# Tail of a mixture of experts: the order of the last sums, and which chunk of tokens is normed first

## The chip, the cores and the metric

The kernel runs on one core of a Trainium2 chip, in one launch. Its time is device microseconds of that core, from the runs shown: the median of three was 709.67 us (709.59 to 709.87). Engines are named as the profile names them: PE is TensorE (PEld its weight loads), DVE is VectorE, ACT is ScalarE, POOL is GpSimd, SP is SyncE, which here only issues DMAs.

## What is computed

Two layers of a perceiver-like model over 512 tokens (8 x 64) of width 256. Each of the six steps adds to the residual `x`. The change lies where the third step ends and the fourth begins:

```python
x = x + _L0_ffn_ref(_layernorm(x), keys, w1, b1, w2, b2, rw, rb)
x = x + _L1_xattn_ref(_layernorm(x), ctx_1024, ctx_1024, mask, gamma, beta)

def _L0_ffn_ref(...):                # mixture: 16 experts, 4 of them for each token
    topv, topi = jax.lax.top_k(logits, TOP_K)
    w = jax.nn.softmax(topv, axis=-1)
    hidden = gelu(jnp.einsum('bld,efd->blef', x, w1) + b1)
    exp_out = jnp.einsum('blef,edf->bled', hidden, w2) + b2
    return jnp.sum(w[..., None] * jnp.take_along_axis(exp_out, topi[..., None], axis=2), axis=2)

def _L1_xattn_ref(q, k, v, mask, gamma, beta):
    logits = jnp.where(mask == 0, NEG, jnp.einsum('bsd,btd->bst', q, k) / 16)
    x = jnp.einsum('bst,btd->bsd', softmax(logits), v)
    return layernorm(x) * gamma + beta
```

## The kernel before, in words

The 512 tokens are four chunks of 128 rows (`TC` = 4), numbered 0 to 3; `X[:, t, :]` is the residual of chunk t. Each engine has its own program, and semaphores alone tie them. Each engine runs its instructions in the order written, so an instruction that waits holds up all behind it on that engine.

**The mixture.** Tokens are sorted by expert into 31 tiles of 128 rows (`TILES`), 8 slices of hidden width each (`UNITS`). PE does the up product of a slice, ACT the gelu, PE the down product, which adds into a bank of `DOWN_BANKS`. The output of tiles 0 to 28 goes to DRAM (`store_tile`, L994) and comes back row by row: `gather_rows(t)` (L999), four indirect DMAs on POOL's queue for each chunk, one for each of a token's four experts. The last two tiles (`LAST` = 2, from `COLD` = 29 on) don't take that way: ACT copies them out (`take_last`, L1292, semaphore `last_taken`), and PE multiplies them with matrices of the tokens' shares (`spreadT`).

**The sums.** Four accumulators, `sums_of(t)`, of 256 columns, two to a bank, take for each chunk the bias (`begin_sums`: gates by `b2`) and the shares of the last two tiles (`add_last(0)` and `add_last(1)`). Before, each of the three does all four chunks at once. `bias_done` counts the banks that are finished: the first holds chunks 0 and 1, the second 2 and 3.

**Chunks become ready on DVE.** `combine(t)` (L1992) is four multiply-adds of gathered rows, `add_sums` (L2020) adds the accumulators, `norm_begin` is the statistics of the layer norm, of which POOL takes the power minus one half (`rstd_of(4, t)`, L702), and `arrive(t)` norms the chunk (L1570) and adds `beta` to the residual (L2027).

**The attention that follows** works chunk by chunk, p = 0 to 3. PE: `turn_tokens` (transposes, L2563), `open_scores` (the mask), `score2` (scores with the context `ctxT2`), `turn2` (transposes of the weights, L2754), `mix2` (product with the context `ctxN2`). ACT: `take_tokens` (copies the transposes, L1256), `weights2` (the exponential, L1329), `take_weights` (L1336). DVE: `greatest` (row maximum, L1998), `normalise` and `leave` (the norm after it and the next layer's). The orders that matter, each of them fixed: DVE has greatest(0), combine(2), greatest(1), arrive(2), combine(3), arrive(3), normalise(0), leave(0), greatest(2). ACT has weights2(2) ahead of take_tokens(3). PE has score2(2), mix2(1), then chunk 3's transposes and score2(3).

**DMAs.** SP issues `ctxT2[2]` (L601) and `ctxN2[1]` (L605), 2 MB each, when all four gathers of chunk 2 have landed, and the last three contexts when `combine(3)` is through and both banks of sums are.

**Filling products.** `keep_running(bank, times)` multiplies constants of 512 columns into a bank that nobody reads. Before, two of them stand behind `add_last(1)`, and one behind `open_scores(0)`.

Of the kernel before, what the change touches and what calls it, by code (L numbers as in the profile page):

```python
# [24 lines left out]
TC = TOK // P  # L25
# [131 lines left out]
def build(nc, d, out):  # L157
    ctx = ExitStack()
    with ctx:
# [536 lines left out]
        def _(pool):  # L696
# [299 lines left out]
            def gather_rows(t, places=range(TOP0)):  # L996
                for j in places:
                    k = TOP0 * t + j
                    nc.gpsimd.indirect_dma_start(y_rows[:, k, :], None, y_slots, bass.IndirectOffsetOnAxis(slots[:, k:k + 1], 0))\  # L999
                        .then_inc(gathered[t], 16)  # L1000
# [16 lines left out]
                pool.wait_ge(y_stored[k], y_stores(k))  # L1017
            gather_rows(0)
            gather_rows(1)
            pool.wait_ge(last_taken, last_before + LAST)  # L1020
            gather_rows(2, range(2))
            rstd_of(4, 0)
            gather_rows(2, range(2, 3))
            rstd_of(4, 1)
            gather_rows(2, range(3, TOP0))
            gather_rows(3)
# [527 lines left out]
        def _(dve):  # L1554
# [431 lines left out]
            for i in range(COLD + 2, TILES):  # L1986
                take_rows(i)

            def combine(t):
                dve.wait_ge(gathered[t], 16 * TOP0)  # L1990
                for j in range(TOP0):
                    order.step(nc.vector.scalar_tensor_tensor(X[:, t, :], y_rows[:, TOP0 * t + j, :], gate_top[:, t, j:j + 1],  # L1992
                                                              X[:, t, :], ALU.mult, ALU.add))

# [28 lines left out]
            def arrive(t):  # L2023

                norm_tile(4, t)
                dve.wait_ge(xn_ready, norm_of(4, t))
                order.mark(nc.vector.tensor_tensor(X[:, t, :], X[:, t, :], part(rows, ROWS, "beta"), ALU.add))  # L2027
# [4 lines left out]
                norm_tile(5, p)  # L2032

            combine(0)
            combine(1)
            add_sums(0, 1)
            norm_begin(4, 0)
            add_sums(1, TC)
            norm_begin(4, 1)
            arrive(0)  # L2040
            arrive(1)
            greatest(0)
            combine(2)
# [236 lines left out]
        def _(pe):  # L2280
# [405 lines left out]
            def sums_of(t):  # L2686
                return pb(SUM_BANKS[t // 2])[:, (t % 2) * D:(t % 2 + 1) * D]

            def begin_sums():
                pe.wait_ge(gateT_ready, 1)  # L2690
                pe.wait_ge(loaded["b2"], 16)
                for t in range(TC):
                    mm(sums_of(t), gateT[:, t, :], b2[:], t % 2 == 0, False)

            def add_last(k):
                pe.wait_ge(last_taken, last_before + k + 1)
                for t in range(TC):
                    done = mm(sums_of(t), spreadT[k][:, t, :], y_tile[(COLD + k) % YB][:], False, k == LAST - 1 and t % 2 == 1)
                    if k == LAST - 1 and t % 2:
                        done.then_inc(bias_done, 1)  # L2700
# [6 lines left out]
            for n in range(TILES * UNITS):  # L2707
                i, u = divmod(n, UNITS)
                if n == REST_AT:
                    dispatch_rest()  # L2710
                if u == (ROW_TURN_AT if i + 1 == HOT else 2) and HOT <= i + 1 < TILES:
                    turn_rows(i + 1)
                if n in SPREAD_AT:
                    turn_spread(SPREAD_AT.index(n))
                if i == COLD and u == 0:
                    turn_gates()
                if i == COLD and u == UNITS - 1:
                    begin_sums()
                if i > COLD and u == UNITS - 2:
                    add_last(i - 1 - COLD)  # L2720
                if n + AHEAD < TILES * UNITS:
                    up(n + AHEAD)
                down(n)

            add_last(LAST - 1)
            keep_running(4, 2)

            def open_scores(p):
                k = p % 2
# [42 lines left out]
                score2(p)  # L2772

            open_scores(0)
            keep_running(4, 1)
            turn_tokens(4, 0, EARLY_BANKS)
            score2(0)
            next_scores(1)
# [372 lines left out]
```

## Time and profile before

| | |
|---|---|
| median of three runs | 709.67 us |
| the profiled execution's own time | 709.58 us |
| its span, first to last instruction | 707.8 us |
| around the span | 1.8 us |
| PE busy | 677.5 us (96%) |
| DVE, POOL, ACT busy | 542.9, 451.5, 413.9 us |
| mean granted clock of PE | 0.998 |

A busy share is an average over stages with different limits. The stage of the change runs from about 478 to 540 us into the span; it is read with the chain of waits, the timelines of the engines, the DMA landings, and the stretches with their granted clock.

### The profile page before, as it was taken

The page shows a single profiled execution, that of the slowest core. Times are in us where ns is not written, and L with a number is a line of the kernel's source. Part 1 is how long each engine was busy: PE and PEld are TensorE (multiplying, and loading weights), DVE is VectorE, ACT ScalarE, POOL GpSimd, SP SyncE. Part 2 cuts the span into 40 slices and gives each one's busy share as a digit, 9 for nine tenths or more (in the row PEclk, how much of TensorE's full clock was granted, in tenths as well). Part 3 has the DMA queues.
Part 4 walks back from the last instruction along what each step waited for, and adds up shares of the span by engine and source line. Part 5 has one row for each costly group of instructions (what it writes and reads, how often), then busy time and mean ns, then how long its engine had stood idle before and what let it go on. Part 6 is the DMA issues. An engine that isn't in the chain of part 4 may idle for free.

```text
span 707.8 us, 15581 instructions
## 1 busy us (share of the span) xinstructions
PE 677.5 (96%) x5734; PEld 556.2 (79%) x5734; DVE 542.9 (77%) x1211; ACT 413.9 (58%) x791; POOL 451.5 (64%) x487
## 2 busy tenths in 40 slices
PE   6899999999999989999999999999999899999998
PEld 3677778777777778999999999997457456666787
DVE  5877878787889766677777777754657999998676
ACT  3665656656665553566666666652346886665441
POOL 4748635556487643798998787736315699898130
PEclk9999999999999999999999999999999999999999
DMA  8301101011006566899998999985874710001000
GB/s 350 124 2 61 61 1 59 2 57 60 0 0 239 210 241 257 295 352 408 421 379 335 352 336 332 351 317 201 332 299 157 258 44 1 1 0 46 1 0 31
DMA packets 20365, 123.38 MB, mean 174 GB/s; under 512 B 2304, under 2 KB 6672, under 8 KB 13008
## 3 DMA queue, kind: packets, MB, share of 16 engines
q1 hardware_dynamic: 17376, 114.59, 42.2%
q0 software_dynamic: 2928, 8.00, 3.1%
q8 instruction: 35, 0.57, 0.3%
q14 instruction: 26, 0.21, 0.1%
HBM read 111.77 MB, written 10.81 MB: 173 GB/s over the span
## 4 chain that ended last, share of the span: by engine, by line
PE 82%; DVE 8%; ACT 5%; issue 2%; POOL 1%; DMA 1%; DVEq 0%; SPq 0%; ACTq 0%; PEldq 0%; POOLq 0%
PE banks L2282 70%; PE banks L2350 8%; DVE shown L2148 2%; PE banks L2918 2%; ACT probs L1156 1%; DVE negmax_raw L1678 1%; PE banks L2591 1%; ACT banks L1449 1%; DVE banks L2155 1%; DVE xn L1570 1%; DMA table<-in_table 1%; PE banks L2754 0%; ACT turned_back L1460 0%; POOL q_heads_hi L714 0%; DVE V L1638 0%
## 5 line engine op out<-in xcount | busy, mean ns | idle before, releaser
L2282 PE MATMUL banks<-xT,raw 128*128 128x128 f32 x992 | 150.5, 275 | 0.6 <-ACT xT L1268 0.6
L2282 PEld LDWEIGHTS banks<-xT,raw 128*128 128x128 f32 x992 | 133.7, 191 | 3.0 <-issue 1.2
L972 POOL TENSOR_TENSOR w_lo<-raw,w_hi 128x1024 fp32r<-128x1024 f32 x52 | 122.8, 2385 | 0.5
L1310 ACT ACTIVATE banks<-banks,later 128x128 f32<-128x128 f32 x208 | 70.5, 339 | 58.3 <-PE banks L2282 57.0
L1942 DVE CAST mid_hi<-banks 128x128 fp32r<-128x128 f32 x208 | 60.0, 289 | 36.5 <-ACT banks L1310 34.4
L1186 ACT ACTIVATE probsT<-banks 128x512 f32<-128x512 f32 x68 | 40.1, 597 | 75.0 <-PE banks L2350 74.7
L1056 POOL TENSOR_TENSOR inject<-BCbc,drive 128x1024 f32<-128x1024 f32 x31 | 72.8, 2362 | 11.3 <-DVE shown L2148 6.5
L1156 ACT ACTIVATE probs<-banks,negmax 128x1024 f32<-128x1024 f32 x64 | 71.2, 1112 | 11.6 <-DVE negmax L1680 9.8
L1678 DVE TENSOR_REDUCE negmax_raw<-banks 128x1 f32<-128x1024 f32 x64 | 77.5, 1211 | 0.5 <-PE banks L2282 0.5
L2282 PE MATMUL banks<-w_hi,mid_hi 128*128 128x256 f32 x208 | 75.5, 363 | 0.0
L2350 PE MATMUL banks<-table,probs 128*128 128x128 f32 x512 | 69.6, 279 | 0.4 <-DVE probsT L1651 0.4
L2350 PEld LDWEIGHTS banks<-table,probs 128*128 128x128 f32 x512 | 55.1, 141 | 16.8 <-issue 14.0
L1944 DVE TENSOR_TENSOR mid_lo<-banks,mid_hi 128x128 fp32r<-128x128 f32 x208 | 60.6, 291 | 7.1
L2282 PE MATMUL banks<-w_hi,mid_lo 128*128 128x256 f32 x208 | 58.6, 282 | 0.0
L2282 PE MATMUL banks<-w_lo,mid_hi 128*128 128x256 f32 x208 | 58.5, 281 | 0.0
L1279 ACT ACTIVATE w_hi<-raw 128x1024 fp32r<-128x1024 f32 x52 | 54.6, 1050 | 0.0
L735 POOL TENSOR_TENSOR ctx_lo<-ctx_raw,ctx_hi 128x1024 fp32r<-128x1024 f32 x14 | 34.3, 2450 | 22.9 <-ACT ctx_hi L1142 22.8
L1449 ACT ACTIVATE banks<-delta,exp_a 128x512 f32<-128x512 f32 x64 | 41.6, 683 | 8.0 <-DVE shown L2165 6.0
L1651 DVE COPY probsT<-banks 128x512 f32<-128x512 f32 x60 | 41.2, 687 | 1.5 <-PE banks L2350 1.5
L1632 DVE SCALAR_TENSOR_TENSOR k_lo<-banks,bk,k_hi 128x512 fp32r<-128x512 f32 x32 | 23.8, 746 | 21.5 <-ACT k_hi L1148 21.5
L2282 PE MATMUL banks<-probsT,V 128*32 128x128 f32 x1024 | 40.0, 277 | 0.0
L2282 PEld LDWEIGHTS banks<-w_hi,mid_hi 128*128 128x128 f32 x208 | 40.0, 192 | 0.0
(363 smaller groups left out, 1710.9 us busy)
## 6 DMA issues: line engine op xcount, KB each, us to landing
raw<-in_w SPq DMA_DIRECT2D x31, 2048.0 KB, 10.6
ctx_raw<-in_ctxT SPq DMA_DIRECT2D x8, 1024.0 KB, 4.8
ctxT<-in_ctxT SPq DMA_DIRECT2D x4, 2048.0 KB, 8.7
ctxN<-in_ctxN SPq DMA_DIRECT2D x4, 2048.0 KB, 13.8
x_slots<-zero SPq DMA_DIRECT2D x1, 3968.0 KB, 12.5
y_slots<-y_tile POOLq DMA_DIRECT2D x29, 128.0 KB, 7.0
wf<-in_w SPq DMA_DIRECT2D x9, 384.0 KB, 6.2
BCbc<-bc_rows SPq DMA_DIRECT2D x6, 512.0 KB, 7.3
```

Source lines behind the costliest of these rows:

```text
L972: nc.gpsimd.tensor_tensor(w2_lo[i % WB][:, cols], raw[i % WB][:, EW // 2:][:, cols], w2_hi[i % 2][:, cols].bitcast(F32), ALU.subtract).the ...
L1056: nc.gpsimd.tensor_tensor(inject[g % 2][:], Bbc[:, GS * g:GS * (g + 1), :], over(drive[:, m, :], GS, 1), ALU.mult).then_inc(inject_ready, 1)
L1156: nc.scalar.activation(probs[i % 2][:], two(i % 2), ACT.Exp, bias=negmax[i % 2][:], scale=0.25, accum_out=sums[i // PAIRS][:, i % PAIRS:i ...
L1279: nc.scalar.activation(w2_hi[i % 2][:, cols], raw[i % WB][:, EW // 2:][:, cols], ACT.Copy).then_inc(w2_hi_ready, 1)
L1310: nc.scalar.activation(to, held, ACT.Gelu, bias=b1[:, bass.ds(at + u, 1)]).then_inc(gelu_done, 1)
L1449: last = nc.scalar.activation(two(HELD_BANKS[g % 2])[:, s * TOK:(s + 1) * TOK], delta[:, m, :], ACT.Copy, scale=exp_a[:, at:at + 1])
L1651: nc.vector.tensor_copy(probsT[c][:, 0:KC // 2, j, :], pb(5).rearrange("p (k n) -> p k n", n=P))\
L1678: nc.vector.tensor_reduce(negmax_raw[i % 2][:], two(i % 2), AX.X, ALU.max, negate=True).then_inc(raw_max, 1)
L1942: nc.vector.tensor_copy(mid_hi[n % HB][:], held).then_inc(mid_hi_ready, 1)
L1944: nc.vector.tensor_tensor(mid_lo[n % HB][:], held, mid_hi[n % HB][:].bitcast(F32), ALU.subtract).then_inc(mid_lo_ready, 1)
L2282: return nc.tensor.matmul(o, lhsT, rhs, start=start, stop=stop)
L2350: last = nc.tensor.transpose(pb(banks[half])[:, k * P:(k + 1) * P], probs[i % 2][:, kc * P:(kc + 1) * P], ident)
```

## The change

It does four things.

1. PE: bias and share sums are made for chunks 0 and 1 first. Those of chunks 2 and 3 come behind, in place of the three filling products; the bias product of chunk 2 stands ahead of the wait for ACT's copy of the last tile.
2. DVE: chunk 0's sums are added as soon as its rows are combined, and it is normed after one of chunk 1's four multiply-adds. The other three follow.
3. DVE: the sums of chunk 1 are added apart (256 columns), those of 2 and 3 together (512) after the statistics of chunk 1.
4. POOL: `rstd_of(4, 0)` stands ahead of the wait for the last tile and of all gathers of chunk 2; before, it stood behind two of them.

```diff
@@ POOL
             gather_rows(1)
+            rstd_of(4, 0)
             pool.wait_ge(last_taken, last_before + LAST)
-            gather_rows(2, range(2))
-            rstd_of(4, 0)
-            gather_rows(2, range(2, 3))
+            gather_rows(2, range(3))
             rstd_of(4, 1)
             gather_rows(2, range(3, TOP0))
@@ DVE
-            def combine(t):
+            def combine(t, places=range(TOP0)):
...
             combine(0)
-            combine(1)
             add_sums(0, 1)
             norm_begin(4, 0)
-            add_sums(1, TC)
+            combine(1, range(1))
+            arrive(0)
+            combine(1, range(1, TOP0))
+            add_sums(1, 2)
             norm_begin(4, 1)
-            arrive(0)
+            add_sums(2, TC)
             arrive(1)
             greatest(0)
@@ PE
                 if i == COLD and u == UNITS - 1:
-                    begin_sums()
+                    begin_sums(range(TC // 2))
                 if i > COLD and u == UNITS - 2:
-                    add_last(i - 1 - COLD)
+                    add_last(i - 1 - COLD, range(TC // 2))
...
-            add_last(LAST - 1)
-            keep_running(4, 2)
+            begin_sums([TC // 2])
+            add_last(LAST - 1, range(TC // 2))
+            begin_sums([TC - 1])
+            for k in range(LAST):
+                add_last(k, range(TC // 2, TC))
...
             open_scores(0)
-            keep_running(4, 1)
             turn_tokens(4, 0, EARLY_BANKS)
```

On PE, around the end of the mixture, before (`b,gateT` is a bias product, `y_tile,spreadT` a share product, `raw,mid` a down product, `later,table` a filling product, `mask_add` opens the scores, `table,xn` are transposes, `ctxT,xnT` the scores):

```order
L2282 MATMUL banks<-raw_123,mid_133 128x256
L2282 MATMUL banks<-y_tile_139,spreadT_178 128x256 x4
L2282 MATMUL banks<-raw_123,mid_134 128x256
L2282 MATMUL banks<-raw_123,mid_135 128x256
L2282 MATMUL banks<-y_tile_140,spreadT_179 128x256 x4
L2282 MATMUL banks<-later,table 128x512 x2
L2282 MATMUL banks<-mask_add_216,ident_r 128x512 x2
L2282 MATMUL banks<-later,table 128x512
L2563 MATMUL banks<-table,xn 128x128 x2
L2282 MATMUL banks<-ctxT_203,xnT 64x512 x8
```

And the same place in the change (lines are one or more further down there):

```order
L2283 MATMUL banks<-raw_123,mid_133 128x256
L2283 MATMUL banks<-y_tile_139,spreadT_178 128x256 x2
L2283 MATMUL banks<-raw_123,mid_134 128x256
L2283 MATMUL banks<-raw_123,mid_135 128x256
L2283 MATMUL banks<-b_53,gateT 128x256
L2283 MATMUL banks<-y_tile_140,spreadT_179 128x256 x2
L2283 MATMUL banks<-b_53,gateT 128x256
L2283 MATMUL banks<-y_tile_139,spreadT_178 128x256 x2
L2283 MATMUL banks<-y_tile_140,spreadT_179 128x256 x2
L2283 MATMUL banks<-mask_add_216,ident_r 128x512 x2
L2564 MATMUL banks<-table,xn 128x128 x2
L2283 MATMUL banks<-ctxT_203,xnT 64x512 x8
```

Two share products ahead of the last down products, and two bias products some way above, moved behind them; the three filling products are gone.

On DVE, from the first combine on, before:

```order
L1992 SCALAR_TENSOR_TENSOR X<-y_rows,gate_top,X 128x256 x8
L2020 TENSOR_TENSOR X<-X,banks 128x256
L1558 BN_STATS stats<-X 128x6
L1562 BN_AGGR moments<-stats 128x2
L1566 TENSOR_SCALAR vareps<-moments 128x1
L2020 TENSOR_TENSOR X<-X,banks 128x768
L1558 BN_STATS stats<-X 128x6
L1562 BN_AGGR moments<-stats 128x2
L1566 TENSOR_SCALAR vareps<-moments 128x1
L1570 TENSOR_SCALAR xn<-X,moments,rstd 128x256
```

In the change:

```order
L1991 SCALAR_TENSOR_TENSOR X<-y_rows,gate_top,X 128x256 x4
L2019 TENSOR_TENSOR X<-X,banks 128x256
L1557 BN_STATS stats<-X 128x6
L1561 BN_AGGR moments<-stats 128x2
L1565 TENSOR_SCALAR vareps<-moments 128x1
L1991 SCALAR_TENSOR_TENSOR X<-y_rows,gate_top,X 128x256
L1569 TENSOR_SCALAR xn<-X,moments,rstd 128x256
L2026 TENSOR_TENSOR X<-X,rows 128x256
L1991 SCALAR_TENSOR_TENSOR X<-y_rows,gate_top,X 128x256 x3
L2019 TENSOR_TENSOR X<-X,banks 128x256
L1557 BN_STATS stats<-X 128x6
```

The norm of chunk 0 (`xn`) moved ahead of three of chunk 1's multiply-adds and of all of chunk 1's statistics.

On POOL, from the last store of a tile on, before (the tenth `y_rows` DMA is the second of chunk 2):

```order
L994 DMA y_slots<-y_tile_138 128x256
L999 DMA y_rows<-y_slots,slots 128x256 x10
L702 TENSOR_TENSOR rstd<-vareps,table 128x1
L999 DMA y_rows<-y_slots,slots 128x256
L702 TENSOR_TENSOR rstd<-vareps,table 128x1
L999 DMA y_rows<-y_slots,slots 128x256 x5
```

In the change:

```order
L994 DMA y_slots<-y_tile_138 128x256
L999 DMA y_rows<-y_slots,slots 128x256 x8
L702 TENSOR_TENSOR rstd<-vareps,table 128x1
L999 DMA y_rows<-y_slots,slots 128x256 x3
L702 TENSOR_TENSOR rstd<-vareps,table 128x1
L999 DMA y_rows<-y_slots,slots 128x256 x5
```

Two gathers moved behind the power for chunk 0; the power for chunk 1 stays between the third and the fourth gather of chunk 2.

## Rows read from the trace of the kernel before

**Rows 1.** The page's chain that ended last: shares of the span by engine

```profile
PE 82%; DVE 8%; ACT 5%; issue 2%; POOL 1%; DMA 1%; DVEq 0%; SPq 0%; ACTq 0%; PEldq 0%; POOLq 0%
```

**Rows 2.** Timeline, PE: start, length, instructions, [idle before, what ended it]

```profile
478.54 1.99 PE L2282 MATMUL banks<-b,gateT 16*128 16x256 f32 x8
...
486.27 1.89 PE L2282 MATMUL banks<-y_tile,spreadT 128*128 128x256 f32 x8
...
489.50 1.99 PE L2282 MATMUL banks<-y_tile,spreadT 128*128 128x256 f32 x8 [0.47 <-ACT y_tile L1292]
491.33 1.88 PE L2282 MATMUL banks<-later,table 128*128 128x512 f32 x4
...
494.37 0.39 PE L2563 MATMUL banks<-table,xn 128*128 128x128 f32 x2
495.32 3.65 PE L2282 MATMUL banks<-ctxT,xnT 128*64 128x512 f32 x16 [0.56 <-ACT xnT L1256]
...
514.67 3.65 PE L2282 MATMUL banks<-ctxN,probsT 128*64 128x256 f32 x32
```

**Rows 3.** Timeline, DVE, the same stretch

```profile
486.66 4.23 DVE L1992 SCALAR_TENSOR_TENSOR X<-y_rows,gate_top,X 128x256 f32<-128x256 f32 x8 [10.78 <-DMA y_rows<-y_slots,slots]
490.92 0.42 DVE L2020 TENSOR_TENSOR X<-X,banks 128x256 f32<-128x256 f32 x1
...
493.86 0.41 DVE L1570 TENSOR_SCALAR xn<-X,moments,rstd 128x256 f32<-128x256 f32 x1
...
506.55 2.05 DVE L1992 SCALAR_TENSOR_TENSOR X<-y_rows,gate_top,X 128x256 f32<-128x256 f32 x4 [0.76 <-DMA y_rows<-y_slots,slots]
...
515.20 1.22 DVE L1998 TENSOR_REDUCE stat<-banks 128x1 f32<-128x1024 f32 x1
```

**Rows 4.** Timeline, POOL: chunk 2's first gather, chunk 0's power, two last gathers

```profile
489.71 0.96 POOL L999 DMA_INDIRECT y_rows<-y_slots,slots  x1 [2.72 <-ACT y_tile L1292]
...
492.29 0.57 POOL L702 TENSOR_TENSOR rstd<-vareps,table 128x1 f32<-128x1 f32 x1 [0.37 <-DVE vareps L1566]
...
494.88 0.99 POOL L999 DMA_INDIRECT y_rows<-y_slots,slots  x1 [0.18 <-issue]
...
499.95 0.95 POOL L999 DMA_INDIRECT y_rows<-y_slots,slots  x1 [0.30 <-issue]
```

**Rows 5.** Timeline, ACT, the same stretch

```profile
489.06 0.38 ACT L1292 ACTIVATE y_tile<-banks 128x256 f32<-128x256 f32 x1 [2.99 <-PE banks L2282]
...
516.64 1.11 ACT L1329 ACTIVATE probs<-banks,stat 128x1024 f32<-128x1024 f32 x1 [5.56 <-DVE stat L1999]
517.65 0.19 ACT L1329 ACTIVATION_READ_ACCUMULATOR probs<-banks,stat 128x1 f32 x1
518.74 0.38 ACT L1256 ACTIVATE xnT<-banks 128x256 f32<-128x256 f32 x1 [0.89 <-PE banks L2563]
```

**Rows 6.** Timeline, SP's queue: the context issued when chunk 2's rows have landed

```profile
498.13 0.46 SPq L605 DMA_DIRECT2D ctxN<-in_ctxN  x1
```

**Rows 7.** Line L605 at 498.0 to 498.3, issue to landing

```profile
DMA to landing us min/median/max: 14.3/14.3/14.3
```

**Rows 8.** Line L999 at 499 to 500 (chunk 3's last gathers), issue to landing

```profile
DMA to landing us min/median/max: 6.6/6.6/6.6
```

**Rows 9.** Timeline, PE, the scores of chunk 3

```profile
519.26 3.65 PE L2282 MATMUL banks<-ctxT,xnT 128*64 128x512 f32 x16
```

**Rows 10.** Stretches: busy PE, PEld, DVE, ACT, POOL; granted clock, DMA share, GB/s

```profile
264.00:266.00 2.00, 1.88 (x12) 1.78 (x12) 1.76 (x14) 1.98 (x4) 0.00 (x0) 0.73 1.05 451
266.00:268.00 2.00, 2.00 (x11) 2.00 (x11) 1.46 (x8) 0.88 (x2) 0.00 (x0) 0.50 0.98 418
268.00:270.00 2.00, 1.81 (x15) 1.62 (x14) 1.11 (x3) 0.00 (x0) 0.00 (x0) 0.92 0.96 401
558.00:560.00 2.00, 0.66 (x3) 0.09 (x1) 2.00 (x3) 2.00 (x5) 2.00 (x2) 1.00 0.98 324
```

**Rows 11.** The page's DMA issues: all 16 gathers, median issue to landing

```profile
y_rows<-y_slots,slots POOLq DMA_INDIRECT x16, 2.8
```

More of the change, by code:

```diff
@@ L1987, in _ @@
                 take_rows(i)
-            def combine(t):
+            def combine(t, places=range(TOP0)):
                 dve.wait_ge(gathered[t], 16 * TOP0)
-                for j in range(TOP0):
+                for j in places:
                     order.step(nc.vector.scalar_tensor_tensor(X[:, t, :], y_rows[:, TOP0 * t + j, :], gate_top[:, t, j:j + 1],
@@ L2687, in sums_of, with begin_sums, add_last @@
                 return pb(SUM_BANKS[t // 2])[:, (t % 2) * D:(t % 2 + 1) * D]
-            def begin_sums():
+            def begin_sums(tiles):
                 pe.wait_ge(gateT_ready, 1)
                 pe.wait_ge(loaded["b2"], 16)
-                for t in range(TC):
+                for t in tiles:
                     mm(sums_of(t), gateT[:, t, :], b2[:], t % 2 == 0, False)
-            def add_last(k):
+            def add_last(k, tiles):
                 pe.wait_ge(last_taken, last_before + k + 1)
-                for t in range(TC):
+                for t in tiles:
                     done = mm(sums_of(t), spreadT[k][:, t, :], y_tile[(COLD + k) % YB][:], False, k == LAST - 1 and t % 2 == 1)
```

## The prediction

> **What bounds the kernel now.** I read the chain that ended last first: 82% of the span lies on PE [rows 1], so a gain must let PE go on sooner. Then PE's own timeline where the change lies [rows 2], then DVE's, POOL's and ACT's for who releases PE [rows 3 to 5], then SP's issues and the landings [rows 6 to 8], because contexts and gathered rows share the DMA engines.
>
> At the end of the mixture PE is dense, then waits 0.47 us at 489.50 for ACT's copy of the last tile, does the share sums, and runs filling products from 491.33 until the transposes of chunk 0 at 494.37 [rows 2]. It fills because DVE delivers chunk 0's norm only at 493.86 to 494.27 [rows 3]: DVE combines chunks 0 and 1 together (eight passes from 486.66, 4.23 us), adds sums, and does chunk 1's statistics before it norms chunk 0. POOL's power for chunk 0 was done at 492.29 + 0.57 = 492.86 [rows 4], one us before DVE used it. So at this point DVE's order bounds PE, by some 3 us.
>
> Further on something else bounds. Chunk 3's multiply-adds start at 506.55, when DVE had stood for its gathered rows [rows 3]. From there DVE's fixed order leads to the row maximum of chunk 2 at 515.20; ACT had stood 5.56 us for it when its exponential starts at 516.64 [rows 5]; and ACT's copy of chunk 3's tokens is queued behind that exponential. Before, that queue is harmless: the copy at 518.74 waits for PE's transposes [rows 5], as PE gets there late.
>
> **The change, part by part.**
>
> *PE, sums split.* Half of the bias products (1.99 us for all) and half of the first share products (1.89) leave the path ahead of the last down product [rows 2]: 1.00 + 0.95 = 1.95 us. The last copy on ACT moves from 489.06 [rows 5] to 487.1. The wait of 0.47 is now covered by one bias product (a quarter of 1.99, 0.50). Share products of chunks 0 and 1 start 0.44 behind the copy's start, as 489.50 did behind 489.06: at 487.55, and need half of 1.99. Their bank is finished at 488.55.
>
> *DVE, chunk 0 first.* The gathers of chunk 0 land before anything that changes, so DVE still starts at 486.66. Four passes, half of 4.23, end at 488.77, 0.2 us after the bank is finished: no new wait. Before, POOL's power started 1.37 us after the sums' add (490.92 to 492.29) [rows 3, 4]; so now at 488.80 + 1.37 = 490.17, done at 490.74. One of chunk 1's passes (4.23/8 = 0.53) fits under that latency. Chunk 0 is normed from 490.78 to 491.19 instead of 494.27: 3.1 us sooner.
>
> *PE, the fillers go.* Behind 488.55 PE still has one bias product and four share products, 0.50 + 0.95 + 1.00, until 491.0, and the mask's products. These have no row here; 491.33 to 494.37 held them and three fillers of up to 1.88/2 each [rows 2], which leaves 0.2 to 0.5. So PE is free at 491.2 to 491.5, just when chunk 0 is there. I take 491.3 for the transposes, 3.1 us sooner, and 492.2 for the first scores (495.32 before). What the fillers kept off, an idle PE, does not arise here, since sums stand in their place.
>
> *POOL, the power ahead of the gathers.* Here the change costs. Gathers of chunk 2 could start at 487.5 now, but POOL stands in line for chunk 0's power until 490.74. The first gather issues at 490.92 (0.18 behind the power, as in the row at 494.88), against 489.71 before [rows 4]. With 0.95 + 0.30 for each, three end at 494.39. Then POOL waits for chunk 1's statistics. DVE: chunk 0's norm ends 491.19, `beta` takes about what an add of 256 columns does, 0.42, so 491.65 with gaps; three passes of 0.53 to 493.24; the sum's add and statistics, again 1.37 until the power starts: 494.61, done 495.18. The fourth gather of chunk 2 issues at 495.36 instead of 494.88: **0.48 us later**. All behind it on POOL's queue is as much later: the last gather of chunk 3 at 500.43 instead of 499.95. On SP's queue the two contexts that wait for chunk 2's rows go out 0.48 later too, and the last three, which wait for chunk 3's combine, as well.
>
> Were chunk 1's statistics in time, the delay would be 0.26 (the three gathers' end at 494.39 alone); were the bank of sums half a us late, it would be 1.0. I take 0.48, since each of its terms has its row.
>
> *What then binds.* Chunk 3's last gather took 6.6 us to land [rows 8], just the 499.95 to 506.55 after which DVE starts [rows 3, 4]. Its DMA runs beside the 4 MB of context, and both move by the same 0.48, so I keep the 6.6: combine(3) at 507.03, chunk 2's maximum at 515.68, its exponential on ACT at 517.12, its accumulator read out by 518.32 (517.65 + 0.19, plus 0.48) [rows 5]. Only then ACT copies chunk 3's tokens. PE is there earlier: without other waits `mix2(1)` would start at 514.67 − 3.1 = 511.6 [rows 2]; its context lands at 498.13 + 14.3 = 512.4 [rows 6, 7], 512.9 with the delay, so it ends at 516.6, and PE stands some 1.5 us in front of the last scores. These follow the copy's start by 0.52 (518.74 to 519.26 before [rows 5, 9]): 518.84, against 519.26.
>
> **The sum.** 3.1 us are won at the first scores, 2.7 of them are lost by the last scores: 0.42 remain. Behind that the order is unchanged and PE bound again; no other term is left. The sum is made in the profiled execution, 709.58 us, 0.09 under the median: 709.58 − 0.42 = 709.16, and from the median 709.67 − 0.42 = 709.25. I give **709.2 us**, 0.06% less. A measurement of this kernel can tell about 0.2%, or 1.4 us, from no change.
>
> **A rule against the change.** The granted clock was at 0.73, 0.50 and 0.92 in three stretches from 264 to 270, after PE had run short products with waits between them; over those 6 us it gave away 0.27 x 2 + 0.50 x 2 + 0.08 x 2 = 1.7 us of PE [rows 10]. From 558 to 560 PE worked 0.66 of 2.00 us, and the clock stayed at 1.00 [rows 10]. The new idle in front of the last scores is of that size, so the sum has no term for the clock. The Trainium skill, page "TensorE: Matmul & The Clock Gate", section "Why this matters for your kernels", says that PE must not be left idle between bursts of matmuls lest its clock drop back to the lower level, which speaks for filling products and against taking them out. By the row at 558 the sum stays at 709.2; by that rule it would be rival B.
>
> **The rivals.**
>
> A, *faster: gathers of chunk 3 land sooner.* If the contexts no longer slowed them, 2.8 us (the median of all 16 [rows 11]) would do in place of 6.6: 500.43 + 2.8 = 503.2, DVE's chain 3.3 us earlier than before, and the last scores wait for PE alone: 516.6 + 1.0 for transposes and copy = 517.6, 1.7 us sooner: 708.0. For it: an issue moved by half a us. Against it: the contexts are released by the gather in front, so both move together.
>
> B, *slower: the clock falls* in PE's new idle of 1.5 us, shortly after a wait of 1.3 for the context. It falls to 1.2 GHz, as at 266 to 268, and costs what it cost there, 1.7 us less the 0.42: 710.9. Against: the row at 558.
>
> C, *slower: the sums come late.* If PE's bank of chunk 0 is finished after DVE's 488.77, POOL's power, and with it every gather and both groups of contexts, moves by as much. At 0.42 us late nothing is won. Were none of PE's 1.95 us saved, the bank would be ready at 490.5, 1.7 late: the last scores 1.3 later than before, 711.0. Against: PE waits for nothing else in that stretch, and 0.2 us is spare.
>
> D, *no effect*: the won time is all given back, 709.7. Half a us more delay at POOL does it.
>
> **How the numbers follow.** My forecast, with a delay of 0.26 to 1.0 and so 709.0 to 709.8, D within it: 0.78. A 0.10, B 0.06, C 0.06. The range reaches to A, the likeliest of the others, and on the upper side a little past D: 707.9 to 710.0; it leaves out B and C. Faster than 708.25 is A and a little of larger gains I don't see: 0.13. Slower than 711.09 is only the upper end of B and C: 0.06. The rest, 0.81, is within 0.2%.
>
> **What would show it.** Right: first scores near 492.2; POOL's power for chunk 0 near 490.2 and chunk 2's fourth gather near 495.4; DVE idle until about 507 for chunk 3's rows; ACT's exponential near 517.1 with the copy directly behind; the last scores near 518.8, PE idle in front of them. Wrong: combine(3) before 506, a PE that never stands between 511 and 519, a granted clock under 1.00 there, or DVE waiting for a bank of sums at 488.8.

## The result, and the profile after

The changed kernel took 713.91 us (median of 8 runs, 711.61 to 714.65), the kernel before 709.77 (8 runs, 709.52 to 712.48) beside it: a ratio of 1.0043, 95% interval 1.0028 to 1.0058 (worked out over all runs, not from the two medians). It is slower by 2 to 4 us where 0.42 us less was predicted. The profiled execution of the change is its slowest, 714.65 us, so the distances read from it show the loss at its largest; two of the eight runs took 711.6 and 711.9 us.

That execution reaches the place of the change 2.05 us later than the one of before: the first bias product starts at 480.59 against 478.54 [rows 2]. The low clock that stood from 264 to 268 [rows 10] goes on until 271 there. Executions of the kernel before seem to do the same in part of the runs (those with a mean clock of 0.995 took mostly 710.6 to 712.7 us), and the profiles of two versions of it further down, which are the same program up to that place, show it too (0.52 or lower from 264 to 270 in both). So this is no effect of the change, and it spreads single runs over 2 to 3 us in every kernel here. All that follows is therefore measured **from the first bias product on PE**, as a distance.

PE after the change (start, length, instructions, [idle before, what ended it]):

```profile
480.59 1.13 PE L2283 MATMUL banks<-b,gateT 16*128 16x256 f32 x4
...
489.27 0.69 PE L2283 MATMUL banks<-b,gateT 16*128 16x256 f32 x2
489.89 1.13 PE L2283 MATMUL banks<-y_tile,spreadT 128*128 128x256 f32 x4
...
494.82 3.65 PE L2283 MATMUL banks<-ctxT,xnT 128*64 128x512 f32 x16 [0.56 <-ACT xnT L1255]
...
515.37 3.67 PE L2283 MATMUL banks<-ctxN,probsT 128*64 128x256 f32 x32 [0.99 <-DMA ctxN<-in_ctxN]
...
522.58 5.35 PE L2283 MATMUL banks<-ctxT,xnT 128*64 128x512 f32 x16 [2.69 <-ACT xnT L1255]
...
529.92 3.67 PE L2283 MATMUL banks<-ctxN,probsT 128*64 128x256 f32 x32 [0.53 <-ACT probsT L1335]
```

The first scores come at a distance of 14.23 (16.78 before [rows 2]): 2.55 us are won. The last scores come at 41.99 (40.72 before [rows 9]): all of it is lost again, and 1.27 more. PE has no wait in front of chunk 0's transposes (493.88), so it is its own sums that set the first scores. PE stood 2.69 us in front of them, and they took 5.35 us instead of 3.65, 1.70 more for the same sixteen products. The third mix product (49.33, and 46.34 before, whose row follows) is then 2.99 us late = 1.27 + 1.70 + 0.02, and stays so to the end: 2.05 + 2.99 makes 5.04 of the 5.07 us between the two profiled executions, and 2.99 lies inside the ratio's interval.

```profile
524.88 3.67 PE L2282 MATMUL banks<-ctxN,probsT 128*64 128x256 f32 x32 [0.50 <-ACT probsT L1336]
```

The stretches with the granted clock (length, busy PE, PEld, DVE, ACT, POOL; clock, DMA share, GB/s):

```profile
520.00:522.00 2.00, 0.00 (x0) 0.00 (x0) 1.86 (x7) 1.04 (x2) 0.00 (x1) 1.00 1.02 434
522.00:524.00 2.00, 1.42 (x6) 0.70 (x8) 1.56 (x5) 0.43 (x3) 0.55 (x1) 0.82 0.99 418
524.00:526.00 2.00, 2.00 (x6) 0.61 (x4) 0.42 (x2) 0.00 (x0) 0.55 (x1) 0.50 1.03 434
526.00:528.00 2.00, 2.00 (x9) 0.62 (x6) 0.04 (x1) 0.00 (x0) 0.00 (x0) 0.82 1.01 422
```

After an idle of 2.69 us PE runs most of the last scores at the lower level, 1.2 GHz (0.50), while DMA is as busy as around them.

Who made PE wait stands on DVE, POOL and ACT (columns as above):

```profile
487.34 2.04 DVE L1991 SCALAR_TENSOR_TENSOR X<-y_rows,gate_top,X 128x256 f32<-128x256 f32 x4 [9.41 <-DMA y_rows<-y_slots,slots]
491.13 0.42 DVE L2019 TENSOR_TENSOR X<-X,banks 128x256 f32<-128x256 f32 x1 [1.75 <-PE banks L2283]
...
493.35 0.41 DVE L1569 TENSOR_SCALAR xn<-X,moments,rstd 128x256 f32<-128x256 f32 x1 [0.54 <-POOL rstd L702]
...
496.87 0.15 DVE L1565 TENSOR_SCALAR vareps<-moments 128x1 f32<-128x1 f32 x1
...
510.87 2.05 DVE L1991 SCALAR_TENSOR_TENSOR X<-y_rows,gate_top,X 128x256 f32<-128x256 f32 x4 [5.22 <-DMA y_rows<-y_slots,slots]
...
519.51 1.22 DVE L1997 TENSOR_REDUCE stat<-banks 128x1 f32<-128x1024 f32 x1
```

```profile
492.50 0.74 POOL L702 TENSOR_TENSOR rstd<-vareps,table 128x1 f32<-128x1 f32 x1 [3.86 <-DVE vareps L1565]
493.43 0.99 POOL L999 DMA_INDIRECT y_rows<-y_slots,slots  x1 [0.19 <-issue]
...
497.11 0.57 POOL L702 TENSOR_TENSOR rstd<-vareps,table 128x1 f32<-128x1 f32 x1 [0.16 <-DVE vareps L1565]
497.86 0.99 POOL L999 DMA_INDIRECT y_rows<-y_slots,slots  x1 [0.19 <-issue]
...
502.93 0.95 POOL L999 DMA_INDIRECT y_rows<-y_slots,slots  x1 [0.30 <-issue]
```

```profile
489.38 0.38 ACT L1291 ACTIVATE y_tile<-banks 128x256 f32<-128x256 f32 x1 [2.13 <-PE banks L2283]
...
520.96 1.11 ACT L1328 ACTIVATE probs<-banks,stat 128x1024 f32<-128x1024 f32 x1 [10.38 <-DVE stat L1998]
522.06 0.37 ACT L1255 ACTIVATE xnT<-banks 128x256 f32<-128x256 f32 x1
```

DVE's statistics of chunk 1 before, which [rows 3] leave out:

```profile
493.79 0.15 DVE L1566 TENSOR_SCALAR vareps<-moments 128x1 f32<-128x1 f32 x1
```

Read as distances, before and after [rows 3 to 5]:

| | before | after | moved |
|---|---|---|---|
| DVE adds chunk 0's sums | 12.38 | 10.54 | −1.84 |
| DVE's last step of chunk 1's statistics | 15.25 | 16.28 | +1.03 |
| fourth gather of chunk 2 issued | 16.34 | 17.27 | +0.93 |
| last gather of chunk 3 issued | 21.41 | 22.34 | +0.93 |
| DVE combines chunk 3 | 28.01 | 30.28 | +2.27 |
| DVE's maximum of chunk 2 | 36.66 | 38.92 | +2.26 |
| ACT's exponential of chunk 2 | 38.10 | 40.37 | +2.27 |
| ACT copies chunk 3's tokens | 40.20 | 41.47 | +1.27 |

Between the last gather's issue and the combine it waits for, another 1.3 us come in. Landings of the last two gathers of chunk 3, issue to landing:

```profile
DMA to landing us min/median/max: 6.9/7.4/7.9
```

7.9 for the last one, where it was 6.6 before [rows 8]. (SP's contexts go out 0.92 later, so the distance between contexts and gathers is the same as before.) In the chain of waits (start, length, what) this landing now leads to the last scores:

```profile
502.93 7.91 DMA y_rows<-y_slots,slots
...
522.58 5.35 PE banks L2283 x16
```

### The profile page after: what moved, and what is told of

Its sections match the earlier page's. It is cut to its first block, busy times and chain, and to the rows that moved or that the text cites. A ratio compares the mean times of both kernels' runs of the same rounds, so it can differ in the third digit from the quotient of the medians.

```text
span 712.9 us, 15574 instructions
## 1 busy us (share of the span) xinstructions
PE 680.0 (95%) x5728; PEld 556.2 (78%) x5728; DVE 543.4 (76%) x1212; ACT 413.9 (58%) x791; POOL 451.9 (63%) x487
## 4 chain that ended last, share of the span: by engine, by line
PE 78%; DVE 10%; ACT 4%; issue 3%; POOL 2%; DMA 2%; DVEq 0%; SPq 0%; ACTq 0%; PEldq 0%; POOLq 0%
PE banks L2283 67%; PE banks L2351 8%; DVE shown L2149 2%; PE banks L2921 2%; ACT probs L1155 1%; DVE negmax_raw L1677 1%; DMA y_rows<-y_slots,slots 1%; PE banks L2592 1%; DVE xn L1569 1%; ACT banks L1448 1%; POOL rstd L702 1%; DVE banks L2156 1%; DVE stats L1557 1%; DMA table<-in_table 1%; POOL y_rows L999 1%
```

## The theory and the runs

Theory: DVE does chunk 1's statistics later than before, so POOL's power for chunk 1, and behind it the fourth gather of chunk 2, are later. All gathers of chunk 3 follow on POOL's queue, they land late behind the contexts, and DVE's fixed order carries that through the maximum of chunk 2 to ACT's copy. PE, ahead of all that, stands, and its clock falls. Rivals: the power for chunk 0, put ahead of the gathers on POOL, costs the time; the second context holds up the gathers; the filling products were what kept the clock. Distances are first scores / last scores / third mix, each from one profiled execution; in brackets after a ratio is its 95% interval against the kernel before.

**The change with POOL's order of before**

```diff
+            pool.wait_ge(last_taken, last_before + LAST)
+            gather_rows(2, range(2))
             rstd_of(4, 0)
-            pool.wait_ge(last_taken, last_before + LAST)
-            gather_rows(2, range(3))
+            gather_rows(2, range(2, 3))
             rstd_of(4, 1)
```

> POOL's order is put back to that of before, PE and DVE stay as changed. Distances are counted in the profile from the first bias product on PE, since all ahead of it is the same program: the last scores started 40.72 us behind it before and 41.99 in the change, the third mix product 46.34 and 49.33. My prediction's term (POOL's wait for chunk 0's power delays the gathers): the fourth gather of chunk 2 comes 1 us or more earlier than in the change (17.27 behind the first bias product there), the last scores come at 41 or less, and the time is 1 to 3 us below the change. Theory now (DVE gives chunk 1's statistics late, and the fourth gather stands behind chunk 1's power, wherever chunk 0's power stands): the fourth gather at 17.0 to 17.5 as in the change, the last scores at 41.5 to 42.5, no difference in time.

712.73 us, 1.0028 [1.0014, 1.0041]; distances 14.24 / 41.78 / 49.09. POOL's timeline, chunk 1's power and the fourth gather of chunk 2, and PE's last scores:

```profile
497.05 0.57 POOL L702 TENSOR_TENSOR rstd<-vareps,table 128x1 f32<-128x1 f32 x1 [2.65 <-DVE vareps L1566]
497.81 0.99 POOL L999 DMA_INDIRECT y_rows<-y_slots,slots  x1 [0.18 <-issue]
```

```profile
522.35 5.35 PE L2284 MATMUL banks<-ctxT,xnT 128*64 128x512 f32 x16 [2.38 <-ACT xnT L1256]
```

The three gathers ahead are out early, and POOL then stands 2.65 us for chunk 1's statistics: the fourth gather comes at 17.24, as in the change (17.27). For the late gather POOL's edit is not the cause; DVE's order is. Whether POOL's edit adds to the time is not resolved, as the two intervals overlap. The clock fell here too, after an idle of 2.38; three of the twelve runs took 709.75 to 710.48 at a mean clock of 0.997 or 0.998 (0.993 in the profiled one), so it seems not to fall in every execution. The kernel before took 709.5 to 711.2 in its runs at 0.998: in those three runs nothing is lost that could be told from it.

**The change, with filling products in front of the last scores**

```diff
             pe.wait_ge(mixed_taken, 1)
-            next_scores(3)
+            turn_tokens(4, 3, EARLY_BANKS)
+            open_scores(3)
+            keep_running(4, 3)
+            score2(3)
```

> The change, with three filling products of 512 columns in PE's wait ahead of the last scores (2.69 us there, after which the granted clock was 0.82, 0.50 and 0.82 and the scores took 5.35 us in place of 3.65). If that idle lowers the clock: clock 1.00 through these stretches, scores at the same distance (41.5 to 42.5 us from the first bias product) but 3.65 us long, the third mix product at 47.6 in place of 49.33, time 1.5 to 1.8 us below the change. Rival (the clock fell for another reason, as the stretch from 511 on was thin in products anyway): scores again over 5 us and no gain.

711.66 us, 1.0019 [1.0011, 1.0028]; 14.23 / 41.74 / 47.35.

```profile
519.63 2.74 PE L2283 MATMUL banks<-later,table 128*128 128x512 f32 x6
522.30 3.65 PE L2283 MATMUL banks<-ctxT,xnT 128*64 128x512 f32 x16
```

```profile
520.00:522.00 2.00, 2.00 (x6) 0.76 (x4) 1.56 (x6) 1.22 (x3) 0.55 (x1) 1.00 1.00 422
522.00:524.00 2.00, 2.00 (x9) 0.63 (x10) 1.13 (x4) 0.00 (x0) 0.55 (x1) 1.00 1.03 434
```

```profile
520.84 0.37 ACT L1255 ACTIVATE xnT<-banks 128x256 f32<-128x256 f32 x1
```

With the idle filled the clock stays at 1.00 and the scores take 3.65; the third mix is 1.01 behind that of before, instead of 2.99. Nine of the eleven runs had a mean clock of 0.997 or 0.998, and none of the change's eight. What is left of the loss is of another kind here. Chunk 3's last gather landed in 6.7:

```profile
DMA to landing us min/median/max: 6.7/6.7/6.7
```

The combine came at 29.09, and ACT's copy at 40.28; the scores follow a copy by 0.52, so they could have begun at 40.80, where they begin before (40.72). It was the filling products, 0.9 us too many, that kept them until 41.74. So without them, by this profile, the won 2.55 us would have been given back to within 0.1, with an idle of some 1.6 us, and if the clock held, near the forecast. That is worked out, not measured.

**PE's part alone** (DVE and POOL as before; bias and share products split and placed as in the change, no filling products)

```diff
...
-            add_last(LAST - 1)
-            keep_running(4, 2)
+            begin_sums([TC // 2])
+            add_last(LAST - 1, range(TC // 2))
+            begin_sums([TC - 1])
+            for k in range(LAST):
+                add_last(k, range(TC // 2, TC))
...
             open_scores(0)
-            keep_running(4, 1)
```

> Only PE's part of the change: sums of chunks 0 and 1 first, no filling products; DVE and POOL as before. Theory (the loss comes from DVE's order, which delays chunk 1's statistics and by them the gathers): fourth gather of chunk 2 at 16 to 16.5 us behind the first bias product as before (16.34), last scores at 40.7, third mix product at 46.3, time within 0.5 us of before, if PE's idle where the fillers were (about 2.5 us) does not lower the clock; if it does, up to 1.7 us more. Rival (the loss comes from PE's part: the second bank's sums late, or the fillers missing): last scores at 41.5 or later with the gathers as before, and time near the change's.

711.02 us, 1.0006 [0.9993, 1.0018], runs from 709.15 to 713.03; 17.27 / 42.90 / 48.52 in its profile.

```profile
495.81 0.44 PE L2563 MATMUL banks<-table,xn 128*128 128x128 f32 x2 [2.82 <-DVE xn L1570]
496.82 5.35 PE L2282 MATMUL banks<-ctxT,xnT 128*64 128x512 f32 x16 [0.56 <-ACT xnT L1256]
```

PE gets through its sums sooner and then stands for DVE's norm of chunk 0, as it stood in filling products before. The idle of 2.82 us now sits ahead of the first scores, and it is these that run slow (5.35). The gathers were not quite as before: DVE stood 0.67 us for chunk 1's rows in this execution, and the fourth gather came at 16.83 (16.0 to 16.5 expected). The last scores (42.90, 40.7 expected) are as late as the first scores (0.49) and the clock (1.70) make them, and PE does not wait in front of them. Four of the five runs at a clock of 0.998 took 709.15 to 709.6: by these, this part changes nothing without the fall.

**The change, gathers ahead of chunk 1's power on POOL**

```diff
-            rstd_of(4, 0)
             pool.wait_ge(last_taken, last_before + LAST)
-            gather_rows(2, range(3))
+            gather_rows(2, range(2))
+            rstd_of(4, 0)
+            gather_rows(2, range(2, TOP0))
+            gather_rows(3, range(1))
             rstd_of(4, 1)
-            gather_rows(2, range(3, TOP0))
-            gather_rows(3)
+            gather_rows(3, range(1, TOP0))
```

> The change with another order on POOL: two gathers of chunk 2, chunk 0's power, the other two and the first of chunk 3, then chunk 1's power and the last three gathers. Theory (gathers behind powers are what is lost): the fourth gather of chunk 2 at about 14.2 us behind the first bias product in place of 17.27, the last gather at about 19.8 in place of 22.34, last scores at 39.5 in place of 41.99, PE's wait ahead of them 0 to 1.5 us so that the clock stays at 1.00, third mix product at 45 to 45.5, time 3 to 4.5 us below the change and about 1 us below before. Rival (chunk 3's rows are held up by the contexts, whatever their issue): combine of chunk 3 and last scores move by less than 1 us.

707.95 us, 0.9970 [0.9957, 0.9983]; 14.24 / 38.40 / 44.04, from a first bias product at 479.46. POOL's fourth gather of chunk 2 and last of chunk 3, DVE's combine, PE's last scores:

```profile
493.60 0.97 POOL L999 DMA_INDIRECT y_rows<-y_slots,slots  x1 [0.30 <-issue]
...
499.29 0.95 POOL L999 DMA_INDIRECT y_rows<-y_slots,slots  x1 [0.31 <-issue]
```

```profile
506.14 2.05 DVE L1992 SCALAR_TENSOR_TENSOR X<-y_rows,gate_top,X 128x256 f32<-128x256 f32 x4 [1.97 <-DMA y_rows<-y_slots,slots]
```

```profile
517.86 3.65 PE L2284 MATMUL banks<-ctxT,xnT 128*64 128x512 f32 x16 [0.32 <-ACT xnT L1256]
```

The fourth gather is 3.13 us earlier than in the change (14.14), the last one 2.51 (19.83), the combine 3.60 (26.68), the last scores 3.59, more than the 2.5 expected: the last gather also landed in 6.8 and not in 7.9. PE waits 0.32 and keeps its clock. This version beats both kernels: with the gathers out first, what PE wins at the first scores lasts to the end.

**The change, chunk 2's maximum earlier on DVE**

```diff
             normalise(0)
+            greatest(2)
             leave(0)
...
-            greatest(2)
             normalise(1)
```

> The change, with one move on DVE: the row maximum of chunk 2 stands ahead of the statistics and norm of chunk 0 for the next layer (leave(0)), no longer behind them. Distances from the first bias product on PE. Theory (the last scores wait for DVE's chain from chunk 3's rows over this maximum, and ACT's exponential): gathers and the combine of chunk 3 as in the change (29 to 30.3 us), the maximum about 1.8 us earlier (37.1 in place of 38.92), last scores at 40.0 to 40.5 in place of 41.99, PE's wait ahead of them near 1 us, granted clock 1.00, third mix product at 45.7 to 46.2 (49.33 in the change, 46.34 before), time about 3 us below the change and 0 to 0.6 below before. Rival (something else holds the last scores, the context's landing or PE): scores at 41.5 or later.

709.52 us, 0.9989 [0.9977, 1.0001]; 14.24 / 40.05 / 45.70, from 480.35.

```profile
517.34 1.22 DVE L1997 TENSOR_REDUCE stat<-banks 128x1 f32<-128x1024 f32 x1
```

```profile
519.88 0.37 ACT L1255 ACTIVATE xnT<-banks 128x256 f32<-128x256 f32 x1
```

```profile
520.40 3.65 PE L2283 MATMUL banks<-ctxT,xnT 128*64 128x512 f32 x16 [0.49 <-DMA ctxT<-in_ctxT]
```

The gathers and the combine are as late as in the change (22.35, 30.29), yet the maximum comes 1.93 us sooner and the last scores 1.94. So DVE's fixed order is what carries the late rows to PE. Chunk 3's context now ties with the copy: it lands at 520.33 (issued at 512.83, 7.5 us), and the copy's start plus the usual 0.52 is 520.40. The time is no longer above that of before, and the interval does not show it below.

**The same order of gathers on the kernel before**

```diff
             pool.wait_ge(last_taken, last_before + LAST)
             gather_rows(2, range(2))
             rstd_of(4, 0)
-            gather_rows(2, range(2, 3))
-            rstd_of(4, 1)
-            gather_rows(2, range(3, TOP0))
-            gather_rows(3)
+            gather_rows(2, range(2, TOP0))
+            gather_rows(3, range(1))
+            rstd_of(4, 1)
+            gather_rows(3, range(1, TOP0))
```

> The kernel before, with POOL's order of the fourth run (both chunk 2's last gathers and chunk 3's first ahead of chunk 1's power). Theory (before, PE sets the last scores, so earlier rows of chunk 3 are worth nothing until PE is early too): last gather at 20.2 us in place of 21.41, combine of chunk 3 about 1.2 earlier, last scores at 40.6 to 40.8 as before, time within 0.1%. Rival (the fourth run's gain is that of the gathers alone): last scores at 39.5 and time 1 us or more below before.

710.88 us, 1.0004 [0.9994, 1.0014]; 16.95 / 40.89 / 46.51. The fourth gather of chunk 2 is 0.37 sooner (15.97), the last gather 0.37 later (21.78), not 1.2 sooner as expected: it stands behind the same two powers and seven gathers as before, POOL waits only 0.38 us for the first of the powers and not for the second, and two of the gathers took 1.13 and 1.22 us where the others of chunk 2 and 3 take 0.95 to 0.99. Chunk 3's rows did not come earlier, so what earlier rows would be worth in that kernel is not tested; what the run shows is that the order by itself is worth nothing there. PE goes into the last scores without a wait, at 522.00, as it does before [rows 9]: PE is the late one in that kernel.

**The change, second context held back until chunk 3's rows have landed**

```diff
             context_T(2)
+            sp.wait_ge(gathered[3], 16 * TOP0)
             context_N(1)
```

> The change, with the second of the two contexts that SP issues (ctxN of chunk 1, 2 MB) held back until chunk 3's rows have landed. If the contexts hold the gathers up: the last gather lands in 3 to 5.5 us in place of 7.9, combine of chunk 3 at 25.5 to 28 us from the first bias product in place of 30.28; the context itself comes 5 to 8 us later and PE then waits for it ahead of the second mix product (34.78 in the change), until 37 or later, so that the time may well be worse than the change's. Rival (a gather of chunk 3 takes 6.5 us or more whatever else moves): combine of chunk 3 at 29.5 or later.

714.03 us, 1.0048 [1.0032, 1.0064]; 14.24 / 44.74 / 50.39. The last gathers still land in 6.3 to 7.6 us, the combine comes at 29.98 (30.28 in the change), and PE stands for the context it now misses, and is slow behind it (6.12 us, 3.67 in the change):

```profile
518.44 6.12 PE L2284 MATMUL banks<-ctxN,probsT 128*64 128x256 f32 x32 [3.90 <-DMA ctxN<-in_ctxN]
```

This number is the rival's, not the theory's. With one context of 2 MB in front the gathers are as slow as with two; between these two profiles the second makes 0.3 us, less than the landing differs between executions (7.9 in the change, 6.7 with filling products). No run issues these gathers with neither context out, so that the first one holds them up is read from the timing alone.

**DVE's and POOL's parts alone** (PE as before, with its filling products)

```diff
...
-            begin_sums([TC // 2])
-            add_last(LAST - 1, range(TC // 2))
-            begin_sums([TC - 1])
-            for k in range(LAST):
-                add_last(k, range(TC // 2, TC))
+            add_last(LAST - 1)
+            keep_running(4, 2)
...
             open_scores(0)
+            keep_running(4, 1)
```

> DVE and POOL as changed, PE as before (all sums for four chunks at once, three filling products). Theory (POOL's gathers hang on chunk 0's sums, by the chain sums, power, chunk 1's passes and statistics, power): the add of chunk 0's sums at 12.0 to 12.2 us in place of 10.54, fourth gather of chunk 2 at 18.7 to 19 in place of 17.27, last scores at 43 to 43.7, a wait of over 2 us ahead of them, clock falls, third mix product at 50 to 51, time 1 to 1.5 us above the change. Rival (PE's part is what costs): time within 0.5 us of before.

711.59 us, 1.0025 [1.0013, 1.0038]; 16.77 / 42.29 / 47.91.

```profile
490.71 0.42 DVE L2019 TENSOR_TENSOR X<-X,banks 128x256 f32<-128x256 f32 x1 [0.75 <-PE banks L2283]
...
509.10 2.05 DVE L1991 SCALAR_TENSOR_TENSOR X<-y_rows,gate_top,X 128x256 f32<-128x256 f32 x4 [3.34 <-DMA y_rows<-y_slots,slots]
```

```profile
520.81 3.65 PE L2283 MATMUL banks<-ctxT,xnT 128*64 128x512 f32 x16 [1.05 <-ACT xnT L1255]
```

The sums come late to DVE, as in rival C: it adds them at 12.19. The gathers move with it, the fourth of chunk 2 to 18.92 and the last to 23.99, and the combine to 30.58. The last scores are 1.57 later than before, less than was expected, and with an idle of 1.05, not over 2, the clock did not fall; by the ratios the time lies under that of the change, where 1 to 1.5 us above was expected. Put beside the change's profile, PE's part brings the last scores forward by 0.30 us (42.29 to 41.99), but the last gather landed in 6.6 here and in 7.9 there. Beside the run with filling products, where it landed in 6.7, it would be 1.49 (to 40.80, worked out above), about as much as the gathers move (1.65). Either way DVE's chain sets the last scores, PE's part adds to PE's wait (1.05 to 2.69 in these two profiles), and behind the longer wait the clock was lower.

**The change with both other orders** (gathers first, and the maximum earlier: the two diffs above together)

> The change with both reorderings, POOL's of the fourth run and DVE's of the fifth. Theory (with the fourth run's order PE itself nearly sets the last scores, its wait there being 0.32 us): last scores at 38.1 to 38.4 us from the first bias product, third mix product at 43.7 to 44.1 (44.04 in the fourth run), time within 0.4 us of the fourth run's and 2 to 3 us below before. Rival (the gain of the two orders adds up): third mix product below 43, time 1 us or more below the fourth run's.

708.57 us, 0.9965 [0.9951, 0.9978]; 14.24 / 38.18 / 43.80. The same as with the gathers alone, within the intervals. Once PE hardly waits, DVE's order costs it only 0.2 us.

**The kernel before without its three filling products**

```diff
             add_last(LAST - 1)
-            keep_running(4, 2)
...
             open_scores(0)
-            keep_running(4, 1)
```

> The kernel before without its three filling products, nothing else. If PE's idle alone lowers the clock: PE waits some 2.3 us for chunk 0's norm, granted clock at 0.50 behind it, first scores at 16.8 us from the first bias product but 5.3 us long in place of 3.65, third mix product at 48.0 in place of 46.34, time 1 to 1.7 us above before. Rival (the third run's clock fell for the order of its sums, and fillers do nothing): first scores 3.65 us long, third mix product at 46.3, time as before.

711.42 us, 1.0017 [1.0002, 1.0032]; 16.58 / 40.52 / 46.14. PE's transposes of chunk 0, and two stretches around them:

```profile
496.15 0.44 PE L2563 MATMUL banks<-table,xn 128*128 128x128 f32 x2 [2.17 <-DVE xn L1570]
```

```profile
494.00:496.00 2.00, 0.00 (x0) 0.00 (x0) 1.90 (x6) 0.00 (x0) 1.69 (x4) 1.00 0.24 68
...
498.00:500.00 2.00, 2.00 (x12) 0.86 (x10) 0.00 (x0) 0.00 (x0) 1.69 (x2) 1.00 0.35 98
```

PE stood 2.17 us, and the clock stayed at 1.00: expected was a fall. The first scores took 3.65, and the third mix product came at 46.14, as before (46.34). Two of the twelve runs show a mean clock of 0.989 and 0.990 and took 714.4 and 714.5 us, longer than twenty of the twenty-one runs of the kernel before that its ratio rests on. Whether it is this idle that lowers the clock in those two is not shown, as only one execution has a profile. Without the filling products the kernel is about 0.2% slower (0.02 to 0.32%); what makes it so is not shown.

## Why the prediction was wrong

Three terms of the sum failed: the delay of the fourth gather, 0.48 in the sum, measured 0.93; the landing that was kept at 6.6 us, measured 7.9; and the clock, put at nothing, measured 1.70. Together that is about 3.5 us. The difference in the profile is 3.41 (2.99 more where 0.42 less was forecast), as ACT's copy came 1.10 and not 1.20 behind the start of the exponential.

**"PE, sums split" was right in kind, and a little too large.** ACT's last copy came 1.73 us sooner (10.52 to 8.79), not 1.95: four bias products take 1.13 together, more than half of 1.99. The one bias product that covers the wait for ACT's copy stands at 489.27, the share products 0.62 behind it, not 0.50. DVE adds chunk 0's sums at 10.54 where 10.26 was expected; it waited for the bank there, for which the prediction had left 0.2 us to spare. (That DVE's row shows a wait of 1.75 us is because the rows of chunk 0 had landed sooner in this execution: DVE began to combine at a distance of 6.75, against 8.12 before.) The bank's 0.28 us are rival C, in small, and one of the signs that the prediction had named for being wrong. The first scores won 2.55 of the 3.1.

**"POOL, the power ahead of the gathers … Here the change costs" had the place and half the size.** The fourth gather of chunk 2 came 0.93 later, not 0.48; of the 0.45 between them 0.28 is the late bank, and 0.17 the power for chunk 0, which took 0.74 and not 0.57. And the heading names the wrong edit: with POOL's order undone the delay is the same, because the power for chunk 1 waits for DVE, which does chunk 0's norm and `beta` ahead of it now.

**"What then binds" named the right chain and kept a landing that did not keep.** Rows of chunk 3, DVE's order up to the maximum of chunk 2, ACT's exponential, the copy behind it: the runs show each link (the earlier maximum brings the last scores forward by 1.94 with the rows as late as ever, the earlier gathers by 3.59). But "I keep the 6.6" failed: it was 7.9 in this execution. Its reason held, contexts and gathers did move together (0.92 and 0.93), but the landing did not follow from it; it is 6.7 and 7.9 in two executions with the same issues at the same distances. The combine came 2.27 later (0.93 + 1.3) where 0.48 was expected, and the last scores 1.27 later instead of 0.42 sooner. This is the first of the two terms that turned the sign. Where the last gather landed in 6.7 (the change with filling products) ACT's copy was in time for scores at 40.80, about where they stand before. So the landing decides how long PE stands, between a change that is given back and one that loses, and the clock adds to the second.

**"A rule against the change" is where the other was left out.** PE's idle was put at 1.5 us, and the clock's fall was given to rival B, with 0.06. The idle was 2.69, as the chain behind was later, and the fall cost 1.70 us; the price B had named, 1.7, was right. The stretch from 558 to 560 [rows 10], on which the zero rested, holds an idle of 1.34 us (the rest of its 2.00), half as long as this one. In the profiles 1.05 and 1.34 us left the clock alone, 2.17 too; after 2.38, 2.69, 2.82 and 3.90 it was lower. A granted clock under 1.00 there was another of the prediction's own signs of being wrong. That filling the idle keeps the clock is shown by the run with filling products; the kernel before without its own kept it in its profile all the same. The Trainium skill (page "TensorE: Matmul & The Clock Gate", section "Why this matters for your kernels") warns of idle gaps between bursts of matmuls, but of longer ones than the 1.5 us expected or the 2.69 us measured, so its rule as it stands does not lead to rival B, though the prediction says so. Where page and measurement differ, the measurement decides: here the clock was lower after 2.38 us.

**The rivals.** A fell: the gathers did not land sooner behind the contexts, with one context in front no more than with two. A's time, 708.0, was met (707.95) by the order with the gathers first, but in another way, and so by chance: there the gathers are issued earlier and land no faster (6.8). B came about, on top of a delay that it did not count. C came about as far as said above; in full, with none of PE's part, it brought the last scores 1.57 later than before (1.3 in C) at a ratio of 1.0025. D's breakeven, some 0.4 us more delay at POOL, was just reached there (0.45), and the landing took the time past it.

## What to carry to other kernels

Time won at one engine is worth what the slowest chain behind it lets through: here 2.55 us came to nothing until the gathers were issued ahead of the small operation that held their queue, and then the change was worth 0.3%. When products are moved into the place of filling ones, ask what the engine does once it arrives early: an idle of 2.4 us or more in front of a dense stretch was paid twice in the profiles, as waiting and as 1.7 us of lower clock (more behind 3.90). And a landing time read where transfers compete belongs to that moment; give it a range, not the value of the row.

## What the runs showed of the hardware

From chunk 1's last gather on, a gather lands in 2.6 to 3.0 us (3.5 and 3.6 once each) while the two contexts that SP issues behind chunk 2's rows are not yet out, and in 6.2 to 7.9 when it is issued about with the first of them or behind it, in every profile here. In the change the gather issued at 500.42, 0.26 ahead of SP's context, already took 6.8; the DMA share rose from 0.25 (498 to 500) to 1.00 (504 to 506). The gathers of chunks 0 and 1 that follow the context before show the same: 6.3 to 7.2 us right behind its issue where the view gives it, and 3.2 to 3.7 some 7 us later. That agrees with what the Trainium skill says on the page "DMA: Bandwidth & Descriptors", section "Issuing engines are not separate DMA queues": transfers of all engines run on the same DMA engines and mix. Why the last gather took 6.2 to 7.1 us in eight of the profiles and 7.6 to 7.9 in four (the change, the change with POOL's order of before, with the maximum earlier, with the second context held back), stays open. The change with filling products has the same issues at the same distances, and 6.7: of the 1.3 us that the landing added, the profiles do not tell what is the kernel's and what the execution's.

After an idle of 2.4 to 3.9 us the clock was lower in four of four profiles, after 2.17 us it was not. (In the runs with 2.82 and 2.17, two transposes and 0.56 us more of waiting stand between the idle and the scores.) The runs without a profile suggest that it falls in part of the executions of one and the same kernel: those with POOL's order of before and those of PE's part alone fall apart into some at a mean clock of 0.997 to 0.998 and some at 0.993 to 0.995. What decides in a given execution was not tried.
